# Attention outputs turned two head groups at a time with 36 columns of the identity

## The reference

```python
x = x + layernorm(attention(layernorm(x)))      # 16 heads of 8 channels
x = x + layernorm(moe(layernorm(x)))            # 8 experts, 2 per token, and a shared one

# attention
qkv = (x @ w_qkv.T + b_qkv)                     # q, k: elu + 1, then rotary embedding
attn = softmax(q @ k.T / sqrt(8))               # per head, 512 x 512
out = attn @ v                                  # per head, 512 x 8
return out + lepe(v)                            # lepe: 3-tap depthwise convolution over tokens
```

## Time and profile before

| | |
|---|---|
| median of 3 runs | 1276.27 us |
| the profiled execution | 1274.32 us, its span 1272.4 us |
| TensorE, VectorE busy | 1076.0 us (85%), 1075.7 us (85%) |
| ScalarE, GpSimd busy | 948.7 us (75%), 854.7 us (67%) |
| matmul instructions | 6504 |
| VectorE instructions | 2480 |
| maxima of the scores, line 1077 | 1024, 649.8 us |
| exponentials, line 972 | 986 seen, 535.5 us |
| V products, line 771 | 2048 records, 273.2 us |
| attention stage | until about 884 us of the span |

### The profile page before, as it was taken

How to read it: one execution, slowest core, us unless ns; L and a number is a source line. 1 busy time by engine, 2 the same in 40 slices (tenths; PEclk the granted TensorE clock), 3 DMA queues, 4 the chain that set the end, 5 groups by cost and what they waited for, 6 DMA issues and landing times. The chain is left out here.

```text
span 1272.4 us, 22262 instructions
## 1 busy us (share of the span) xinstructions
PE 1076.0 (85%) x6504; PEld 463.7 (36%) x6504; DVE 1075.7 (85%) x2480; ACT 948.7 (75%) x1752; POOL 854.7 (67%) x1134
## 2 busy tenths in 40 slices
PE   1499999999999999999999999898899999888900
PEld 0112222222322322223223232232677778666600
DVE  2398899999999999999999999972786888999944
ACT  1118888888888888888788888788788888777612
POOL 5445466676678887887878878553555645888675
PEclk9559999999999999999999999999899999988855
DMA  2553432423523334325234234103134644445322
GB/s 67 118 125 130 98 80 67 110 74 75 118 78 102 89 107 110 100 72 126 78 102 102 85 94 103 46 17 125 37 98 141 210 132 139 138 144 150 100 62 80
DMA packets 108985, 128.22 MB, mean 101 GB/s; under 512 B 14225, under 2 KB 81845, under 8 KB 108597
## 3 DMA queue, kind: packets, MB, share of 16 engines
q1 hardware_dynamic: 98848, 105.94, 30.7%
q0 software_dynamic: 8192, 16.79, 4.9%
q10 hardware_dynamic: 1824, 4.06, 0.9%
HBM read 58.85 MB, written 59.51 MB: 93 GB/s over the span
## 5 line engine op out<-in xcount | busy, mean ns | idle before, releaser
L1077 DVE TENSOR_REDUCE MX<-psS 128x1 f32<-128x512 f32 x1024 | 649.8, 679 | 62.6 <-PE psS L757 56.9
L972 ACT ACTIVATE PR<-psST 128x512 f32<-128x512 f32 x986 | 535.5, 599 | 113.2 <-PE psST L745 112.2
L757 PE MATMUL psS<-KS,QS 48*128 48x512 bf16 x1024 | 366.0, 400 | 36.0 <-DMA KS<-scratch_parts 23.7
L745 PE MATMUL psST<-QS,KS 51*128 51x512 bf16 x986 | 336.5, 385 | 37.8 <-ACT PR L972 21.6
L771 PE MATMUL psPV<-PR,V 128*32 128x512 f32 x2048 | 273.2, 605 | 7.8 <-ACT SHARED L886 1.5
L745 PEld LDWEIGHTS psST<-QS,KS 51*128 51x128 bf16 x986 | 78.8, 93 | 389.5 <-ACT PR L972 373.1
L1968 POOL DMA_INDIRECT SHARED<-scratch_y,FROM x128 | 130.7, 1021 | 43.6 <-issue 35.3
L462 POOL DMA_INDIRECT scratch_x<-XN,POSI x128 | 130.8, 1022 | 36.3 <-issue 33.5
L757 PEld LDWEIGHTS psS<-KS,QS 48*128 48x128 bf16 x1024 | 87.5, 93 | 90.7 <-DVE MX L1077 60.8
L1506 PE MATMUL psH<-XH,WS 128*128 128x512 f32 x164 | 73.8, 450 | 1.8 <-ACT XH L1598 0.8
L771 PEld LDWEIGHTS psPV<-PR,V 128*32 128x32 f32 x2048 | 40.8, 108 | 80.7 <-issue 61.7
(11 more groups left out here) (213 smaller groups left out, 1958.4 us busy)
## 6 DMA issues: line engine op xcount, KB each, us to landing
scratch_parts<-PT SPq DMA_DIRECT2D x192, 128.0 KB, 2.4
QS<-scratch_parts SPq DMA_DIRECT2D x64, 192.0 KB, 3.6
KS<-scratch_parts SPq DMA_DIRECT2D x64, 192.0 KB, 4.6
XR<-scratch_x SPq DMA_DIRECT2D x46, 256.0 KB, 2.8
scratch_y<-YR SPq DMA_DIRECT2D x46, 256.0 KB, 2.1
RES<-EL SPq DMA_DIRECT2D x64, 128.0 KB, 2.0
scratch_x<-ZERO SPq DMA_DIRECT2D x18, 256.0 KB
X<-in_x SPq DMA_DIRECT2D x16, 256.0 KB, 5.1
```

The costliest lines, as they stand in the source:

```text
L745: nc.tensor.matmul(bank(st_banks(t), k)[:], KS[t.par][rows, h // 2, kc * P:(kc + 1) * P], QS[t.par][rows, h // 2, :], start=True, stop=Tru ...
L757: nc.tensor.matmul(bank(psS, k)[:], QS[b.par][rows, h // 2, qc * P:(qc + 1) * P], KS[b.par][rows, h // 2, :], start=True, stop=True).then_ ...
L972: nc.scalar.activation(PR[:, s % 2, j, :], bank(st_banks(t), k)[:], ACT.Exp, scale=SCALE).then_inc(st_exp, 1)
L1077: nc.vector.tensor_reduce(out=MX[:, qc, h:h + 1], in_=bank(psS, k)[:], axis=AX.X, op=ALU.max).then_inc(s_max, 1)
```

## The change

- `turn_heads` takes a half hf (two groups) instead of a group g. It waits until both groups of the half are in OT. For each of four pieces of 128 tokens and each of two groups it makes an ordinary matmul instead of a transpose: the OT piece as stationary operand, and as moving operand PICKED, the 36 columns of the identity that are in use (nine of each 32). The 288 results per token lie densely in the bank.
- `normalise` works on a half: one reciprocal of 4 x 8 sums, and one product of 4 x 8 x 8 outputs. REC is twice as wide.
- Groups 0 and 1 are turned in slot 10 and normalised in slot 11; groups 2 and 3 in slot 4 of the next iteration and normalised in slot 5. The turns in slots 7 and 14 and the normalisations in slots 8 and 15 are gone.
- MISC has 12 uses instead of 14; the order and readers of the psM banks follow.
- `copy_heads` waits until the previous turn of the same half is done. For groups 2 and 3 that is slot 10's turn, for group 1 slot 4's; for group 0, copied in slot 4, it is the turn made in that same slot.
- At the seam, the turn and the normalisation of the last batch take groups 2 and 3.

```diff
-        self.REC = sb("REC", [P, QC, HG], F32)
+        self.REC = sb("REC", [P, QC, HALF], F32)
+        self.PICKED = IDF[:].rearrange("p (j v) -> p j v", v=VW)[:, :, 0:D + 1]
...
-    def turn_heads(self, pe, b, g, m):
+    def turn_heads(self, pe, b, hf, m):
         nc = self.nc
-        pe.wait_ge(self.ot_ready, b.done(4, g + 1))
+        pe.wait_ge(self.ot_ready, b.done(4, 2 * hf + 2))
+        wide = HG * (D + 1)
         for qc in range(QC):
-            last = nc.tensor.transpose(m[:, qc * P:(qc + 1) * P], self.OT[:, g % 2, qc * P:(qc + 1) * P], self.IDF[:])
+            for g in range(2):
+                at = wide * (2 * qc + g)
+                last = nc.tensor.matmul(m[:, at:at + wide], self.OT[:, g, qc * P:(qc + 1) * P], self.PICKED,
+                                        start=True, stop=True)
         last.then_inc(self.oT_psum, 1)
...
-        MISC = ["xT", "q", "k", "mT1", "O3", "O0", "lepeT", "mT0", "O1", "vT", "xT2", "V",
-                "O2", "lg"]
+        MISC = ["xT", "q", "k", "mT1", "O23", "lepeT", "mT0", "O01", "vT", "xT2", "V", "lg"]
...
                 if s == 4 and prev.live:
-                    misc_freed(pe, t, "O3")
-                    ends.turn_heads(pe, prev, 3, misc_bank("O3"))
-                if s == 7 and t.live:
-                    misc_freed(pe, t, "O0")
-                    ends.turn_heads(pe, t, 0, misc_bank("O0"))
+                    misc_freed(pe, t, "O23")
+                    ends.turn_heads(pe, prev, 1, misc_bank("O23"))
...
                 if s == 10 and t.live:
-                    misc_freed(pe, t, "O1")
-                    ends.turn_heads(pe, t, 1, misc_bank("O1"))
+                    misc_freed(pe, t, "O01")
+                    ends.turn_heads(pe, t, 0, misc_bank("O01"))
...
-                if s == 14 and t.live:
-                    misc_freed(pe, t, "O2")
-                    ends.turn_heads(pe, t, 2, misc_bank("O2"))
...
             def copy_heads(b, g):
 
                 act.wait_ge(pv_done, b.done(16, 4 * g + 4))
-                if due(before := b.done(4, g - 1)):
+                if due(before := b.done(2, g // 2)):
                     act.wait_ge(oT_psum, before)
...
                 if s == 5 and j == 3 and prev.live:
-                    ends.normalise(dve, prev, 3, misc_bank("O3"))
-                if s == 8 and j == 1 and t.live:
-                    ends.normalise(dve, t, 0, misc_bank("O0"))
+                    ends.normalise(dve, prev, 1, misc_bank("O23"))
...
                 if s == 11 and j == 1 and t.live:
-                    ends.normalise(dve, t, 1, misc_bank("O1"))
-                if s == 15 and j == 1 and t.live:
-                    ends.normalise(dve, t, 2, misc_bank("O2"))
+                    ends.normalise(dve, t, 0, misc_bank("O01"))
```

More of the change, by code:

```diff
@@ L246, in store_turned, with normalise @@
         sp.dma_start(self.XTD[b.number()], self.XT2[:, b.par, :]).then_inc(self.xT2_stored[b.par], 16)
-    def normalise(self, dve, b, g, bank):
+    def normalise(self, dve, b, hf, bank):
         nc = self.nc
-        m = bank[:].rearrange("p (q j v) -> p q j v", q=QC, j=HG)
-        dve.wait_ge(self.oT_psum, b.done(4, g + 1))
-        if due(before := b.done(4, g)):
+        m = bank[:, 0:QC * HALF * (D + 1)].rearrange("p (q j v) -> p q j v", q=QC, j=HALF)
+        dve.wait_ge(self.oT_psum, b.done(2, hf + 1))
+        if due(before := b.done(2, hf)):
             dve.wait_ge(self.o_norm, before)
         nc.vector.reciprocal(self.REC[:], m[:, :, :, D]).then_inc(self.recip, 1)
-        dve.wait_ge(self.recip, b.done(4, g + 1))
-        if g == 0:
+        dve.wait_ge(self.recip, b.done(2, hf + 1))
+        if hf == 0:
             if due(before := b.done(1, -1)):
                 dve.wait_ge(self.z_ready, before)
-        y = self.Y[:, b.par, :, g * HG * D:(g + 1) * HG * D].rearrange("p q (j d) -> p q j d", j=HG)
-        nc.vector.tensor_tensor(y, m[:, :, :, 0:D], self.REC[:].unsqueeze(3).to_broadcast([P, QC, HG, D]),
+        y = self.Y[:, b.par, :, hf * HALF * D:(hf + 1) * HALF * D].rearrange("p q (j d) -> p q j d", j=HALF)
+        nc.vector.tensor_tensor(y, m[:, :, :, 0:D], self.REC[:].unsqueeze(3).to_broadcast([P, QC, HALF, D]),
                                 ALU.mult).then_inc(self.o_norm, 1)
@@ L266, in add_lepe @@
         dve.wait_ge(self.lepeT_psum, b.done(1, 1))
-        dve.wait_ge(self.o_norm, b.done(4, 4))
+        dve.wait_ge(self.o_norm, b.done(2, 2))
         self.nc.vector.tensor_tensor(self.Y[:, b.par], bank[:].rearrange("p (q c) -> p q c", q=QC),
@@ L570, in attention @@
         READER = {"xT": (2, xT_ready, 1, 1), "mT1": (0, mT_ready, 2, 2), "q": (2, qk_elu[0], 1, 1),
[L571 to L575, removed]
+                  "O23": (-1, o_norm, 2, 2), "k": (2, qk_elu[1], 1, 1), "lepeT": (-1, y_ready, 1, 1),
+                  "mT0": (1, mT_ready, 2, 1), "O01": (0, o_norm, 2, 1), "V": (1, v_ready, 1, 1),
+                  "vT": (1, vT_ready, 1, 1), "xT2": (-2, xT2_ready, 1, 1), "lg": (-2, lg_read, 1, 1)}
         def misc_freed(pe, t, use):
@@ L1533, in drain @@
                 if p == 0:
-                    pe.wait_ge(ends.o_norm, last.done(4, 4))
+                    pe.wait_ge(ends.o_norm, last.done(2, 2))
                     ends.turn_lepe(pe, last, psG)
@@ L1561, in drain @@
                     turn_gates(QC - 1, psG)
-            ends.turn_heads(pe, Batch(B - 1), 3, psG)
+            ends.turn_heads(pe, Batch(B - 1), 1, psG)
             take(0)
@@ L1855, in _ @@
             turn(0)
-            ends.normalise(dve, Batch(B - 1), 3, psG)
+            ends.normalise(dve, Batch(B - 1), 1, psG)
             for p in range(END):
```

## The result

| | before | changed |
|---|---|---|
| median | 1276.62 us (1275.63 to 1277.93, 4 runs) | 1307.34 us (1306.22 to 1310.22, 4 runs) |
| ratio | | 1.0243 (95%: 1.0224 to 1.0263), slower |
| profiled execution, span | 1274.3, 1272.4 us | 1307.97, 1306.0 us |
| start of the last copy out of psPV (end of the attention stage) | 883.4 us | 917.3 us |
| from there to the end | 389.0 us | 388.7 us |

The forecast was 1288.0 (1275 to 1301): slower was right, the size was not. All of it lies in the attention stage, +33.9 us where +12.3 was forecast. A ratio is that of several executions; a clock reading or a stretch comes from one execution of each kernel.

What follows compares the result with a forecast made beforehand. VectorE was taken to pace gated iterations, the TensorE-ScalarE round trip through psST's two banks the others. Eight ungated iterations 9.4, t = 0 0.5, five gated 0.5, t = 14 0.6, t = 15 1.3: +12.3 us, 1288 (1275 to 1301).

Steps and rivals of the forecast that it cites:

- The new turn: TensorE, slots 4 and 10: eight products of 36 columns take 1.85 us, so a turn grows by 1.26 us.
- the added wait: Slot 4: ScalarE's copy of group 0 waits for that slot's turn, 16 times, starting near 563.0 instead of 561.79.
- Iterations without gates, +1.2: Iterations without gating steps on VectorE: slot 4 +0.66, slot 10 +0.67, slot 14 -0.15 us; bounds 0.5 to 2.5.
- With gates: Iterations with gating steps, VectorE dense: the delays and savings sum to about +0.1 us, from -0.66 to +1.2.
- the removed normalise of slot 8 gives 0.48 back: VectorE, slot 8 of gated iterations: dropping the normalise there returns 0.48 us against slot 4's delay.
- The 0.6 of delay that reaches VectorE: Gated iterations: slot 4's delay on TensorE reaches VectorE as about 0.6 us.
- The third rival: Added wait and both growths fall in gated iterations too: +19 to +25 us, 1298; chance 0.2.
- gated iterations up by about 1: Sign of the third rival: periods with gates up by 1 us too.
- t = 15: Last batch, ScalarE dense: its group 0 copy waits 1.26 us in slot 4 and never catches up, +1.3 us.
- t = 0 and t = 14: First iteration, with no batch before it, +0.5 us; t = 14, gated but lighter on VectorE, +0.6 us.
- Its own sign of being right: VectorE's busy time down by about 10 us, with its waits for psS up by more.

Runs made afterwards that it cites:

- e2: The kernel before with each of its four turns made as four products of 36 columns instead of four transposes; ratio 1.0094 (1.0039 to 1.0148).
- e12: The changed kernel with four products of 72 columns per turn instead of eight, half the heads' outputs being copies; ratio 1.0058 (1.0022 to 1.0093).
- e14: The kernel before with VectorE's gating (router) steps 7 to 20 moved from slots 6 to 12 to slots 10 to 14; ratio 0.9956 (0.9942 to 0.9969).

## Why the prediction was wrong in size

- **The new turn, the added wait: right.** 1.91 us (1.85). ScalarE's copy waits for the turn 15 times, 17.1 us (16 times forecast).
- **Iterations without gates, +1.2: right but for one.** Measured 1.26 to 1.49, and 1.74 in t = 13. From the turn of slot 4 to that of lepe 12.15 became 12.90 (+0.75, forecast 0.66), slot 10 to the logits 15.74 became 16.35 (+0.61, 0.67), the rest -0.10 (-0.15). Eight of them 10.9 us (9.4).
- **The largest failed step is a term put at nothing: TensorE's clock.** It makes 14.2 of the 33.9 us, and of the 21.6 us by which the stage missed the forecast. The earlier trace rows had 1.00 throughout, and the prediction said nothing of it. Without these 14.2 us the time would have been 1293, inside the range. e2 and e12 show that with turns of 1.0 us there are few falls; those of slots 9 and 10 came only behind waits for VectorE.
- **The other failed step is "With gates": "the removed normalise of slot 8 gives 0.48 back".** Sum about +0.1 was forecast, +0.89 measured, 4.5 us in five gated iterations instead of 0.5. The 0.6 of delay that reaches VectorE was right: from t = 6 to 7 its idle time grew by 0.69. But its busy time, which was to fall by 0.66 a batch, rose by 0.20. Normalise gave 0.43 back; the maxima took 0.28 more, and small instructions, router steps among them, 0.35. In t = 6 slot 4 to lepe grew by 1.03 where 0.6 - 0.48 was forecast: a router step there took 0.54 us longer. The prediction had taken the durations of VectorE's other instructions as fixed. What makes the maxima longer is open.
- The third rival's size (+19 to +25) was nearer, and its sign, gated iterations up by about 1, came in. Its reason did so by half: only slot 4's growth came in there, slot 10's stayed hidden (in t = 6 slot 10 to the logits went from 16.56 to 16.37), and it had no clock either.
- **t = 15: 2.4 us instead of 1.3.** Slot 4 to lepe gave 1.27 as forecast; from slot 10's turn to the last copy another 1.3 came, where the prediction put nothing. That slot 10's growth lies open there because ScalarE is dense in the last batch is argued.
- t = 0 and t = 14 hold what is left, 0.3 and 1.6 us (1.1 forecast for both).
- Its own sign of being right, VectorE's busy time down by about 10 us, did not come: 1075.7 became 1075.9.

Open is what makes the clock fall in one iteration and not in the next with the same waits (t = 8 and 10, not t = 6 and 12, of the changed kernel), and what holds ScalarE on the three slower chips. A turn of 36 columns by true transposes was not tried.

## What to carry to other kernels

Merging two short bursts into one long one can cost more than it saves, even with fewer VectorE instructions: what a slot's hole swallows is per slot. Before counting an engine's saving, list which of its instructions have two durations in the trace (here 0.2 and 0.8 to 1.0 us for one shape): a shift of 0.7 us decided which of them applied. Sum them over the iteration in both kernels, or stretched steps that only moved are taken for added ones. Moving VectorE's two-input steps so that fewer meet GpSimd's products (5.4 instead of 6.2 us for all of them) gained 0.44% (e14) for the edit of one table. And read the granted clock of every run: a stretch can lose more to it than the work that was added.

## What was not expected of the hardware

- TensorE's granted clock fell to 1.2 GHz in a stage where TensorE is 94% busy (47.57 of 50.83 us), in pieces of 3.4 to 10.2 us, behind 1.9 us of small f32 products or behind two waits of 0.4 and 0.5 us. Before such a piece it was 1.00. In nine traces with such turns in slot 4, 37 pieces stand behind them.
- Sixteen f32 records with fresh 128-column weights take 1.91 us with 36 columns, 0.119 each; with 72 columns eight take 1.04 (0.130 each).
- A 128x64 VectorE step with two inputs takes 0.22 us, and 0.79 to 1.14 in the rows above where it starts inside a GpSimd product, until that ends.
